# Waits for landings in GpSimd's indirect transfers of a Mamba + mixture-of-experts layer

## What is computed

```python
x = L0_attn_x
x = _layernorm(x + _L0_attn_ref(x, ...))
# _L0_ffn_ref
gates = jax.nn.softmax(xf @ router_w, axis=-1)
top_v, top_i = jax.lax.top_k(gates, TOP_K)
routed = jax.vmap(lambda rw_, W1_, W2_: _ffn(xf, rw_, W1_, W2_))(rms_w, w1, w2)
routed_out = jnp.einsum('end,ne->nd', routed, masked)
shared = jax.vmap(...)(rms_w_s, w1_s, w2_s).sum(0)
x = _layernorm(x + (routed_out + shared))
```

## Time and profile before

| what | value |
|---|---|
| median of 3 runs | 720.47 us |
| profiled execution, first to last instruction | 769.2 us |
| busy: PE / DVE / POOL / ACT | 651.3 / 596.1 / 501.3 / 444.7 us |
| POOL's returns (L623) | 141, 142.1 us |
| POOL's dispatches (L669) | 128, 143.7 us |
| granted TensorE clock, mean | 0.926 |

### The profile page before, as it was taken

The page is one execution under the profiler, slowest core; times in us unless marked ns, Lnnn a source line. Parts: engine busy times, 40 slices in busy tenths (PEclk is TensorE's granted clock), DMA queues, the critical chain, the costliest instruction groups (busy, mean ns, idle before and its releaser), DMA issues.

```text
span 769.2 us, 14716 instructions
## 1 busy us (share of the span) xinstructions
PE 651.3 (85%) x4299; PEld 554.7 (72%) x4299; DVE 596.1 (77%) x1744; ACT 444.7 (58%) x1225; POOL 501.3 (65%) x545
## 2 busy tenths in 40 slices
PE   5987798999999999999999997965988878767830
PEld 4765576788888888888888886854987768656720
DVE  4999999999999999999999864427447343698875
ACT  4885688867877876787787543411223111346445
POOL 1144565887797897888888776556655656566561
PEclk9999999999999999999999998878889889997865
DMA  8541111211221121111111055114222236536126
GB/s 305 193 138 42 43 43 41 64 57 55 62 64 62 60 62 50 63 64 60 59 50 62 22 167 192 45 55 101 80 80 77 76 80 172 168 100 205 60 80 218
DMA packets 62638, 70.76 MB, mean 92 GB/s; under 512 B 10335, under 2 KB 45285, under 8 KB 62304
## 3 DMA queue, kind: packets, MB, share of 16 engines
q1 hardware_dynamic: 41568, 47.70, 19.6%
q0 software_dynamic: 8608, 16.87, 6.5%
q10 hardware_dynamic: 12384, 5.26, 2.9%
HBM read 48.55 MB, written 23.01 MB: 93 GB/s over the span
## 4 chain that ended last, share of the span: by engine, by line
PE 60%; DVE 13%; issue 12%; ACT 7%; another core or an unknown queue 4%; ACTq 2%; DMA 1%; DVEq 0%; SPq 0%
PE bank L745 7%; PE bank L817 6%; PE bank L826 6%; PE bank L884 6%; PE bank L770 5%; PE bank L800 5%; DVE xbcT_area L1155 3%; PE bank L881 3%; PE bank L871 3%; PE bank L833 3%; PE bank L785 3%; PE bank L888 2%; DVE decay_area L1163 2%; ACT x L933 2%
## 5 line engine op out<-in xcount | busy, mean ns | idle before, releaser
L623 POOL DMA_INDIRECT returned<-xT,slots_in x141 | 142.1, 1008 | 107.6 <-DVE xT L1453 67.3
L669 POOL DMA_INDIRECT dispatched<-rows,row_u x128 | 143.7, 1123 | 33.9 <-issue 31.8
L745 PE MATMUL bank<-xT 128*128 128x128 f32 x564 | 92.0, 316 | 43.4 <-issue 24.9
L1155 DVE SCALAR_TENSOR_TENSOR xbcT_area<-raw,conv_w,xbcT_area 128x512 f32<-128x512 f32 x162 | 123.9, 766 | 2.9 <-ACT xbcT_area L999 2.9
L745 PEld LDWEIGHTS bank<-xT 128*128 128x128 f32 x564 | 82.7, 226 | 50.7 <-issue 42.4
L944 ACT ACTIVATE raw<-bank 128x512 f32<-128x512 f32 (+1 forms) x71 | 39.8, 590 | 126.9 <-remote 61.5
L661 POOL TENSOR_TENSOR state_kept<-state,whole 128x256 f32<-128x256 f32 x56 | 72.1, 1288 | 59.0 <-DVE state L1181 49.1
L1453 DVE COPY xT<-bank 128x512 f32<-128x512 f32 (+1 forms) x36 | 24.3, 676 | 90.5 <-remote 72.8
L770 PE MATMUL bank<-xbcT_area,raw 128*128 x564 | 83.4, 308 | 4.7 <-issue 4.6
L1163 DVE TENSOR_TENSOR_SCAN decay_area<-decay_area,ident_heads 128x512 f32<-128x512 f32 x64 | 85.0, 1329 | 0.0
L770 PEld LDWEIGHTS bank<-xbcT_area,raw 128*128 128x128 f32 x564 | 79.6, 224 | 7.0 <-issue 7.0
(11 more groups left out here) (228 smaller groups left out, 1497.0 us busy)
## 6 DMA issues: line engine op xcount, KB each, us to landing
decay_area<-decay_rows SPq DMA_DIRECT2D x64, 256.0 KB
slots_in<-dispatched ACTq DMA_DIRECT2D x77, 64.5 KB
hid<-returned SPq DMA_DIRECT2D x18, 256.0 KB
slots_in<-dispatched SPq DMA_DIRECT2D x64, 64.5 KB
xT<-xT_dram SPq DMA_DIRECT2D x8, 512.0 KB, 7.9
x<-x_dram SPq DMA_DIRECT2D x8, 512.0 KB, 7.8
out_dram<-x SPq DMA_DIRECT2D x16, 256.0 KB
xT<-returned SPq DMA_DIRECT2D x14, 256.0 KB
```

The source lines that it names most:

```text
L623: e.indirect_dma_start(returned, bass.IndirectOffsetOnAxis(ap=slots_in[sb_][:, n, D:ROW].bitcast(U32), axis=0), slots_out[b][:, n * P:(n + ...
L669: e.indirect_dma_start(dispatched, bass.IndirectOffsetOnAxis(ap=row_u[t % 2][:, m:m + 1], axis=0), rows[t % 3][:, k, c4, :], None).then_in ...
L745: mm = e.matmul(bank[:, off:off + P], w1_now[b][:, k * P:(k + 1) * P], slotsT[gr % len(slotsT)][:, n % 4 * P:(n % 4 + 1) * P], start=True, ...
L1155: e.scalar_tensor_tensor(o, r[:, n:n + W], conv_w[:, k, TAPS - 1 - n:TAPS - n], o, ALU.mult, ALU.add).then_inc(S["conv"])
```

## The change

Three waits are added on POOL; no instruction moves and none is taken away. In `return_rows`, from group 1 on, the first transfer waits until all transfers of the group before have landed, and the third waits until the first two of its own group have. For the dispatches of tiles 13, 14 and 15 each even-numbered transfer waits until every earlier one of its tile (for the first: of the tile before) has landed. So never more than two transfers are in flight there.

```diff
                 on.wait_ge("routed_out", gr + 1)
                 on.wait_ge(f"slots_in{sb_}", 16 * tiles_upto(gr, len(slots_in)))
+                if gr > 0:
+                    on.wait_ge(f"returned{(gr - 1) % len(slots_out)}", 64 * ((gr - 1) // len(slots_out) + 1))
                 for n in range(len(slot_tiles(gr))):
+                    if n == 2:
+                        on.wait_ge(f"returned{b}", 64 * (gr // len(slots_out)) + 32)
                     e.indirect_dma_start(returned, bass.IndirectOffsetOnAxis(ap=slots_in[sb_][:, n, D:ROW].bitcast(U32), axis=0),
...
+            def dispatches_landed(t, m):
+
+                t, m = (t, m) if m > 0 else (t - 1, 8)
+                return f"dispatched{t % 2}", 128 * (t // 2) + 16 * m
...
                     on.wait_ge("row_targets", t + 1)
+                    if t >= NT - 3 and m % 2 == 0:
+                        on.wait_ge(*dispatches_landed(t, m))
                     e.indirect_dma_start(dispatched, bass.IndirectOffsetOnAxis(ap=row_u[t % 2][:, m:m + 1], axis=0),
```

## The result

The changed kernel takes **863.45 us** (median of 4 runs, 859.37 to 868.4), the kernel before 719.05 us beside it (4 runs, 716.99 to 721.0): a ratio of 1.2006, 95% interval 1.1947 to 1.2065. That is +144.4 us, where I had predicted +66; 863 lies outside the range of 740 to 820. The direction was right and the size far too small.

A forecast was written before the change was run, and what follows sets the result against it. POOL's chain of transfer pairs was to bound everything behind the mixer, the last return starting at 483.05 + 77c. The profile-based 720.5 us timed, plus 41.7 for the chain and 24 for the halts, gave 786 us, range 740 to 820.

The forecast's parts named there:

- start of tile 13: Where the change begins to act: tile 13's first dispatch on POOL, taken at 467.85 us as in the profile before.
- c: On POOL, time from a pair's first transfer to the next pair's first: 4.0 us, between 3.49 and 4.33.
- end behind the last return: Time from the last return's start to the kernel's end, 769.2 - 749.3 = 19.9 us, claimed to stay.
- S: What the halts are worth in the difference between timed runs: 24 us, bounds 0 and 33.
- the formula's five cheap steps of 2.54: Five places, at switches between returns and dispatches, where the next pair waits for something long landed: 2.54 us a step.
- the halts: Behind 467 us, stretches where other engines stand still, going together with long runs of POOL's transfers; 33 us counted from rows.
- Rival 1: Landing on POOL's queue cheap and covered: c = 3.49, last return 2.4 us later, 723 us with S = 0; chance 0.07.
- rival 2: Groups 10 to 23: halts are real in every run and pairs end them; c = 3.3 gives 708 us; chance 0.06.
- rival 3: Landings slower under load, beside slot loads and picks: 2.2 us landing, c = 5.2, time 879 us; chance 0.04.

The follow-up runs named there:

- r9: The changed kernel, unchanged, timed again in a set of the long kind: 859.52 us beside a kernel before of 764.58, ratio 1.1262.
- r10: The kernel before with two small GpSimd memsets ahead of every return and no wait for a landing: 821.75 us (one run), kernel before 718.91, ratio 1.143.
- r8: The changed kernel with each pick loading only a quarter of its rows: 849.62 us beside a kernel before of 718.91, ratio 1.1822.
- r12: The kernel before, unchanged, recorded and timed in a set of the short kind: 718.12 us beside 719.18, ratio 0.9995.
- r0: The kernel before, unchanged, recorded and timed in a set of the long kind: 765.0 us beside 765.22, ratio 1.0007.
- r15: The kernel before with one small GpSimd memset ahead of every return, in a set of the long kind: 763.22 us beside 766.01, ratio 0.9955.
- r4: The kernel before plus a wait of each group's third return for the landing of the group before: 764.02 us beside 764.58, ratio 0.9981.
- r2: The kernel before plus only the wait inside groups, ahead of each group's third return: 792.66 us beside 765.22, ratio 1.0362.
- r3: The kernel before plus only the wait between groups, first return for all of the group before: 786.24 us beside 765.22, ratio 1.0293.
- r16: The kernel before plus only the wait between groups, measured again in another long set: 789.11 us beside 766.01, ratio 1.029.
- r6: The changed kernel with the returns' bounds check added to its dispatches: 865.88 us beside a kernel before of 764.58, ratio 1.1347.
- r7: The kernel before with one small GpSimd memset ahead of every return, in a short set: 737.28 us beside 718.91, ratio 1.0257.

## Why the prediction was wrong in its size

The terms, as the prediction put them and as measured, in us:

| term | predicted | measured |
|---|---|---|
| start of tile 13 | 467.85 | 475.14: +7.3 |
| c, mean over 77 steps | 4.0 | (845.82 - 475.14 - 2.5 - 12.7) / 77 = 4.62: +47.5 |
| end behind the last return | 19.9 | 864.8 - 845.8 = 19.0: -0.9 |
| S, profiled execution against timed runs | 24 | (769.2 - 719.05) - (864.8 - 863.45) = 48.8: +24.8 |
| whole change | 41.7 + 24 = 65.7 | 65.7 + 7.3 + 47.5 - 0.9 + 24.8 = 144.4 |

The 12.7 is the formula's five cheap steps of 2.54. S is the gap of the kernel before less that of the changed kernel, whose recorded execution is like its timed runs.

**Right.** The mechanism: POOL's queue became the bound for everything behind the mixer, returns start in pairs, 1.28 us apart (a group every (740.30 - 557.32) / 20 = 9.1 us where I said 8.0) and with the idle time put down to landings; the halts of the earlier trace rows are all but gone, which r9 shows and not the first trace; the end behind the last return stayed, and r10 bears out that the time follows the last return. The landing itself was read rightly from SP's picks: 1.25 to 1.32 us behind the issue's end, measured 2.23 - 0.97 = 1.26 with little beside it. Rival 1 (a cheap landing) and rival 2 (faster by the end of the halts) both needed c at or under 3.5 and are out.

**The step that failed most: c = 4.0.** Of its 0.62 us, 0.27 came from "less a quarter microsecond that SP's start must hold twice". No row showed that anything was held twice, a quarter off 4.33 gives 4.08 and not 4.0, and the restart is a full 0.76, as the row of POOL's own had it. The c of 4.27 with little beside it was inside my bounds. The other 0.35 is in the main load: 0.05 is the longer step between groups (4.37), picks are shown for 0.13 (r8), the rest is not separated. I took 4.33 as the upper end although I knew that its landing rows came from a stretch with few picks and stores, and gave the load a rival of its own at 5.2 with a chance of 0.04. It belonged in the forecast's range; 0.35 of a microsecond 77 times is 27 us. The Trainium skill, DMA: Bandwidth & Descriptors, anatomy of a DMA from GpSimd, gives about 2.0 us fixed plus bytes over 436 GB/s. Its fixed part is setup and completion together, so it counts from the issue. The trace has 2.23 us for 64 KB *from the start of the issue*, not behind its end. Read so, the estimate of 2.15 us by the page agrees; counted from the issue's end, as in rival 3, it gave a c of 5.16, which is too long.

**The second: S = 24.** The bounds were 0 and 33, and the gap of 48.7 stood in the table. I counted 33 us of halts from rows of 498 to 510, 537 and 580 to 660 us, and then took half of the gap because "the 467 us ahead must have a share in it". They have none: r12 reaches tile 13 at 468.02. My rows were right for groups 0 to 4 (11.5 + 4.0 = 15.5, measured 16.5) but covered only part of groups 4 to 24 (17.4 counted, measured 30.9). That the gap bounded the term from above should have made 48.7 the upper end. The cause that I set beside it is not supported either: the Trainium skill, NOTIFIC — the notification-queue block, section 7.1, has producers held back rather than records lost inside the block, but r12 and r0 are recorded executions of both kinds, each like its unrecorded neighbours.

**The third: the first dispatch of tile 13.** My formula starts it at 467.85, its time in the trace of before, so its wait for tile 12's landing was priced at nothing, though SP's two big weight loads go out just ahead of those transfers: 7.3 us in the trace of the table, some 4 over all traces.

Put c = 4.62 into the forecast with the rest as it was, and the sum is 834, outside the range by itself. Put S = 48.8 in alone and it is 811, inside. With both it is 858.5.

**What stays open.** What makes a set of runs halted. It is not the rate of the returns (r15 halts at 1.47 us, r12 does not at 1.28), not the number in flight down to six (r4), and not the recording (r0, r12). Nor does it go by the chip's number: r0, which is halted, and r12, which is not, both ran on number 7. In the halted sets the remote waits (DVE and ACT together) shrink with the transfers that can be in flight between two waits for a landing: 157 and 181 us in the kernel before (rows of *before* and r0), 151 with six in flight (r4), 95 with four (r2), 67 and 66 with four and the wait between groups (r3, r16), 12.6 with two (r9). Whether the number in flight does that, or the pauses that each wait makes, these runs don't separate. r2 still has

```profile
ACT raw L951 <- remote: 46.3, 7, 14.2
```

PE never waits for "remote". Beside DVE's 11.5 us of the earlier trace rows it does single matmuls with idle time that the profile calls "issue", in which it waits for nothing that the profile shows:

```profile
504.93 0.36 PE L817 MATMUL bank<-w_shared,hid 128*128 128x128 f32 x1 [1.15 <-issue]
506.35 0.37 PE L817 MATMUL bank<-w_shared,hid 128*128 128x128 f32 x1 [1.06 <-issue]
```

From 467 to 700 us PE has 36 us of such idle time in the halted trace of before, 37 in r0 and none in r12. That leaves a rival which no run here tests: that in a halted set something holds up the supply of instructions, or the signals between engines, and not one particular transfer. The instruction queues move as many packets in both kinds (36 and 42 or 43), so it isn't their amount.

So the change does in the main what its rival hoped, and pays 94.9 us in the halted sets (859.52 against 764.58), where the halts are worth 46 in all.

## What to carry to other kernels

A wait for the landing of the transfers just issued costs the landing *and* the restart of the queue each time, here 4.3 us for two transfers instead of 2.6, and 4.6 in the mean; before adding one, count how often it falls on a queue that others wait for, and take its price under the load of that stage, not from its quietest row. A wait for something that landed a group ago cost nothing here (r4, in a halted set). And when a profiled execution and the timed runs differ by nearly 7%, they are two different executions: bound every term by the whole gap, or get a profile of the kind that is timed, before adding a forecast to one and comparing with the other.

## What I had not expected of the hardware

- One kernel has two durations, 719 and 765 us, that hold for a whole set of runs; the difference lies wholly behind the first long run of GpSimd's indirect transfers, as waits of DVE and ACT whose releaser the profile can't name, up to 11.5 us long, and as idle "issue" time of PE between single matmuls.
- A bounds check on an indirect transfer costs nothing to be seen while GpSimd's queue runs on (1.28 against 1.27 us from start to start), and 0.5 us a transfer as soon as the queue has to wait for a landing (restart 0.76 against 0.27 us; 0.55 in r6).
- A scatter of 64 KB landed 1.26 us behind its issue, but 3.3 us later with two weight loads and some two dozen slot loads in flight (5.59 against 2.27), and up to 3.9 us later beside picks (idle 5.97 against 2.05).
- An indirect transfer of 128 rows takes 1.28 us of GpSimd, start to start, over 80 transfers in a row (r12): four of them a group were a limit of a kernel whose busiest engine was PE (r7: 0.19 us more a return, 18 us longer).
